# Exact key and query parts in the zeroed rows of the first attention's score products, doubled by transfers

## The reference, cut to what matters

```
def step(state, inp):
    qt, kt, vt, gt = inp
    gate = jnp.exp(gt)
    state = state * gate[..., None] + vt[..., None] * kt[..., None, :]
    out_t = jnp.einsum('bhvk,bhk->bhv', state, qt)
    return (state, out_t)
```

## Time and profile before

| | |
|---|---|
| median of 3 runs | 3458.81 us (3458.78 to 3458.85) |
| the profiled execution | 3460.7 us, span of its trace 3459.0 us |
| PE busy | 3342.5 us, 97% of the span |
| DVE busy | 2607.4 us, 75% |
| ACT busy | 1863.8 us, 54% |
| POOL busy | 1273.4 us, 37% |
| DMA engines | 11.3% on the main queue |

### The profile page before, as it was taken

The page is one execution under the profiler, slowest core; times in us unless marked ns, Lnnn a source line. Parts: engine busy times, 40 slices in busy tenths (PEclk is TensorE's granted clock), DMA queues, the critical chain, the costliest instruction groups (busy, mean ns, idle before and its releaser), DMA issues.

```text
span 3459.0 us, 88576 instructions
## 1 busy us (share of the span) xinstructions
PE 3342.5 (97%) x34556; PEld 2274.0 (66%) x34556; DVE 2607.4 (75%) x6329; ACT 1863.8 (54%) x4135; POOL 1273.4 (37%) x1393
## 2 busy tenths in 40 slices
PE   6999999999999999999999999999999999999998
PEld 3676666766666666666666666666676666766666
DVE  6777867778677777877778777786777867778777
ACT  3364654646546465463655636456364653646546
POOL 4424244242442524325233342423434244242442
PEclk8999999999999999999999999999999999999999
DMA  4001010010110101011010100101001010010110
GB/s 105 18 22 47 24 38 19 24 44 24 38 23 24 40 24 47 14 38 26 24 50 11 50 18 20 49 12 49 18 23 45 24 38 23 20 44 24 38 23 26
DMA packets 98479, 109.59 MB, mean 32 GB/s; under 512 B 21153, under 2 KB 75025, under 8 KB 98065
## 3 DMA queue, kind: packets, MB, share of 16 engines
q1 hardware_dynamic: 93200, 102.25, 11.3%
q10 hardware_dynamic: 4864, 1.69, 0.2%
HBM read 74.01 MB, written 17.30 MB: 26 GB/s over the span
## 4 chain that ended last, share of the span: by engine, by line
PE 75%; DVE 12%; ACT 5%; issue 5%; POOL 1%; DMA 0%; DVEq 0%; SPq 0%; ACTq 0%; POOLq 0%
PE bank L1549 6%; PE bank L1508 5%; PE bank L1879 5%; PE bank L1647 5%; PE bank L1529 5%; PE bank L1781 5%; PE bank L1897 4%; PE bank L1719 4%; PE bank L1664 3%; PE bank L1619 3%; PE bank L1816 3%; PE bank L1842 3%; PE bank L1604 3%; PE bank L1713 2%; DVE am L1245 2%
## 5 line engine op out<-in xcount | busy, mean ns | idle before, releaser
L867 POOL TENSOR_TENSOR qx<-qx 128x512 f32<-128x512 f32 x256 | 277.3, 1088 | 658.7 <-ACT qx L1113 657.8
L1470 DVE TENSOR_TENSOR sq_lo<-qx,sq_hi 128x512 fp32r<-128x512 f32 x256 | 224.1, 875 | 177.1 <-ACT sq_hi L1092 176.6
L1378 DVE TENSOR_REDUCE row_max<-bank 128x4 f32<-128x384 f32 x512 | 270.8, 550 | 95.4 <-PE bank L1781 95.0
L1245 DVE TENSOR_TENSOR am<-bank,causal 128x512 f32<-128x512 f32 x512 | 328.1, 683 | 11.3 <-PE bank L1619 11.3
L988 ACT ACTIVATE tanh_g<-bank 128x256 f32<-128x256 f32 x128 | 49.3, 385 | 394.9 <-PE bank L1508 394.9
L1508 PE MATMUL bank<-w_vg,xt 128*128 128x512 f32 x512 | 252.3, 615 | 0.0
L1549 PE MATMUL bank<-xt,w_down 128*128 128x512 f32 x512 | 237.2, 596 | 0.0
L1897 PE MATMUL bank<-sq_hi,pj_t 128*128 128x512 f32 x512 | 213.2, 416 | 14.8 <-DVE sq_lo L1470 10.3
L1387 DVE TENSOR_TENSOR am<-bank,row_max 128x384 f32<-128x384 f32 x384 | 212.8, 554 | 9.8
L1113 ACT ACTIVATE qx<-bank,scale_fc 128x512 f32<-128x512 f32 x256 | 177.9, 695 | 70.9 <-PE bank L1884 69.0
L1032 ACT ACTIVATE am<-am 128x384 f32<-128x384 f32 x384 | 202.9, 528 | 8.5 <-DVE am L1387 8.5
(11 more groups left out here) (264 smaller groups left out, 8671.4 us busy)
## 6 DMA issues: line engine op xcount, KB each, us to landing
g_wide<-gate_rows SPq DMA_DIRECT2D x64, 512.0 KB, 6.0
x<-in_L_attn_x SPq DMA_DIRECT2D x128, 128.0 KB, 2.3
qt<-in_L_attn_x SPq DMA_DIRECT2D x128, 128.0 KB, 2.6
out<-x SPq DMA_DIRECT2D x128, 128.0 KB, 1.7
k<-k SPq DMA_DIRECT2D x96, 128.0 KB, 2.4
qt<-in_L_attn_x ACTq DMA_DIRECT2D x8, 128.0 KB, 7.6
x<-in_L_ffn_w_fc SPq DMA_DIRECT2D x1, 1024.0 KB, 5.9
attn<-in_L_ffn_w_proj SPq DMA_DIRECT2D x1, 1024.0 KB, 8.7
```

The lines of the kernel that those rows point to most:

```text
L867: nc.gpsimd.tensor_tensor(sq[:, n % 3, :], relu[:, n % 3, :], relu[:, n % 3, :], ALU.mult)\
L1245: nc.vector.tensor_tensor(am_tiles[:, :, j], bank[3 + j][:].rearrange("p (f e t) -> p f e t", f=2, e=2), causal[:].unsqueeze(1).unsqueeze( ...
L1378: nc.vector.tensor_reduce(row_max[:, j, :], bank[1 + j][:, 0:4 * KW].rearrange("p (h k) -> p h k", k=KW), AX.X, ALU.max, negate=(j == 0)). ...
L1470: nc.vector.tensor_tensor(sq_lo[:, n % 3, :], sq[:, n % 3, :], sq_hi[:, n % 3, :].bitcast(F32), ALU.subtract)\
```

## The change

**Scores.** For chunks 1 to 7 the score product is no longer a float32 product with zeros. Keys and queries are split into a high part (rounded to float32r, which TensorE multiplies in one pass) and a low part (the rest, again rounded). Two tiles, `stacked` (the storage of `sq_hi` and `sq_lo`, free in this stage), hold for each chunk three 128x512 parts: `[0]` keys, `[1]` high queries, `[2]` low queries, each twice (`e`, once per head parity). In the copy for one parity, the 16 rows of the other head, which would hold zeros, are overwritten by transfers from the 16 rows next to them: the low keys (`k_low`) into part 0, the same queries into parts 1 and 2. One product over 32 rows then gives (high key + low key) . query part. There are 32 products of 128x128 in float32r for a chunk, instead of 8 of 128x256 in float32. Chunk 0 keeps the old way.

**Work for it.** ACT: `split_highs(c)`, two casts of 128x512. DVE: `split_queries(c)`, one subtraction of 128x512. POOL: `split_keys(c)`, one subtraction of 128x256; `parity_queries` remains for chunk 0 only. SP: `split_moves(c)`, 16 transfers of 16 rows each. PE waits for all 16 (`split_done`). Chunks 1 and 2 are split in chunk 0 (chunk 1's casts just before it), chunk c + 2 in chunk c.

**Seams.** ACT applies an exponential to one column (`warm`) before the last `experts_relu(3)`. DVE's `attention_bias(c-1)` moves for c = 1 and 2 ahead of the last `maxima` and `shifted`. POOL's `head_rstd` moves from after n = 4, 7 to after n = 5, 8, and DVE's normalising from n = 6, 7, 8, 9 to 6, 7, 9, 10.

```diff
-    qp = qx_flat[:, 0:8 * P].rearrange("p (b f e t) -> p b f e t", b=2, f=2, e=2)
+    qp = qx_flat[:, 0:4 * P].rearrange("p (f e t) -> p f e t", f=2, e=2)
+    k_low = qx_flat[:, 4 * P:8 * P].rearrange("p (b f t) -> p b f t", b=2, f=2)
+    stacked = tuple(tile[:].rearrange("p b t -> p (b t)").rearrange("p (i e f t) -> p i e f t", i=3, e=2, f=2)
+                    for tile in (sq_hi, sq_lo))
@@ SP
+                    def split_moves(c):
+                        sp.wait_ge(s["spq_ok"], at("spq_ok", c))
+                        sp.wait_ge(s["spk_ok"], at("spk_ok", c))
+                        tile = stacked[c % 2]
+                        for e in range(2):
+                            for j in range(4):
+                                here = slice(32 * j + DH * e, 32 * j + DH * e + DH)
+                                there = slice(32 * j + DH * (1 - e), 32 * j + DH * (1 - e) + DH)
+                                sp.dma_start(tile[there, 0, e].bitcast(F32), k_low[here, c % 2]).then_inc(split_done[c], 16)
+                                sp.dma_start(tile[there, 1:3, e].bitcast(F32), tile[here, 1:3, e].bitcast(F32)).then_inc(split_done[c], 16)
                     for g in range(NG):
+                        if g:
+                            for c in range(1, 4):
+                                split_moves(c)
...
+                    for c in range(4, NC):
+                        split_moves(c)
@@ POOL
+                    def split_keys(c):
+                        pool.wait_ge(s["sph_ok"], at("sph_ok", c))
+                        nc.gpsimd.tensor_tensor(k_low[:, c % 2].bitcast(F32R), kt[:, :, c * P:(c + 1) * P],
+                                                stacked[c % 2][:, 0, 0].bitcast(F32), ALU.subtract)\
+                          .then_inc(s["spk_ok"], 1)
-                            parity_queries(c + 1)
+                            if c == 0:
+                                split_keys(1)
                             hidden_gated(c + 1)
+                            if c + 2 < NC:
+                                split_keys(c + 2)
-                        if n in (4, 7):
-                            head_rstd(pool, n // 7)
+                        if n in (5, 8):
+                            head_rstd(pool, n // 8)
@@ ACT
                     experts_relu(2)
+                    nc.scalar.activation(warm[:], gdiff[:, 0:1], ACT.Exp)
                     experts_relu(3)
+                    def split_highs(c):
+                        if c >= 3:
+                            act.wait_ge(s["at_ok"], at("at_ok", 4 * c - 4))
+                        cols = slice(c * P, (c + 1) * P)
+                        nc.scalar.copy(stacked[c % 2][:, 1], qt[:, :, cols].unsqueeze(1).broadcast_to([P, 2, 2, P]))
+                        nc.scalar.copy(stacked[c % 2][:, 0], kt[:, :, cols].unsqueeze(1).broadcast_to([P, 2, 2, P]))\
+                          .then_inc(s["sph_ok"], 1)
+                    split_highs(1)
                     for c in range(NC):
+                        if c + 2 < NC:
+                            split_highs(c + 2)
@@ DVE
+                    def split_queries(c):
+                        dve.wait_ge(s["sph_ok"], at("sph_ok", c))
+                        nc.vector.tensor_tensor(stacked[c % 2][:, 2],
+                                                qt[:, :, c * P:(c + 1) * P].unsqueeze(1).broadcast_to([P, 2, 2, P]),
+                                                stacked[c % 2][:, 1].bitcast(F32), ALU.subtract).then_inc(s["spq_ok"], 1)
                         if c + 1 < NC:
                             experts_gate(c)
+                        if c == 0:
+                            split_queries(1)
+                        if c + 2 < NC:
+                            split_queries(c + 2)
...
+                        if 0 < c < 3:
+                            attention_bias(c - 1)
                         maxima(4 * c + 7)
                         shifted(4 * c + 7)
-                        if c:
+                        if c >= 3:
                             attention_bias(c - 1)
@@ PE, parity_scores(c)
-                        pe.wait_ge(s["qx_ok"], at("qx_ok", c + 1))
+                        if c == 0:
+                            pe.wait_ge(s["qx_ok"], at("qx_ok", 1))
+                        else:
+                            pe.wait_ge(split_done[c], at("split_done", 16 * 16))
...
+                        tile = stacked[c % 2]
                         for half in range(2):
-                            for j in range(4):
...
+                            for e in range(2):
+                                for part in range(2):
+                                    for j in range(4):
+                                        rows = slice(32 * j, 32 * j + 32)
+                                        mm = nc.tensor.matmul(bank[3 + j][:, (2 * half + e) * P:(2 * half + e + 1) * P],
+                                                              tile[rows, 0, e, half, :], tile[rows, 1 + part, e, half, :],
+                                                              start=(part == 0), stop=(part == 1), skip_group_check=True)
```

More of the change, by code:

```diff
@@ L113, in build_program @@
     gden = sb("gden", [P, NC])
+    warm = sb("warm", [P, 1])
     g_top = sb("g_top", [P, 2, NC])
@@ L303, in build_program @@
     low_banks = (2, 0)
+    split_done = [sem(f"split_done{c}") for c in range(NC)]
     x_in = [sem(f"x_in{c}") for c in range(NC)]
@@ L327, in build_program @@
             (128, "xc_ok"),
+            (256, "split_done"),
     ):
@@ L1481, in _ @@
                             head_moments(dve)
[L1482 to L1484 removed]
+                        if n in normalise_steps:
+                            p = normalise_steps.index(n)
+                            head_normalise(dve, 2 * p)
+                            head_normalise(dve, 2 * p + 1)
                         if n == NG * MT - 2:
```

45 lines of the change are left out of this document (22 added, 23 removed).

## The result

| | before | after |
|---|---|---|
| median of the runs (least to most), us | 3458.8 | 3724.7 (3721.2 to 3726.6) |
| ratio after/before, 95% interval | | 1.077 (1.075 to 1.079) |
| span of the profiled execution, us | 3459.0 | 3724.4 |
| mean granted clock | 1.00 | 0.96 |
| a sequence, first score product to first score product, us | 212.08 | 228.62 |

The change costs 266 us, 16.6 in each of 16 sequences. I had forecast slower, but 106 us: the direction was right, and the time lies above my range (3690). First the page of the kernel after. The second line is its chain of waits by engine.

What follows compares the result with a forecast made beforehand. PE's nearly gapless list was taken as the bound. Chunk 1 later by 5.0, clock 2.2 and seams -0.6 gave +6.6 us a sequence, +106 us over 16: 3565 us, 8 in 10 between 3495 and 3690.

Steps and rivals of the forecast that it cites:

- products, casts, subtractions: Score products and added work on ACT, DVE and POOL: no gain or loss, 0 us a sequence.
- chunk 0 to 1 longer: PE stands 5.8 us for SP's 16 transfers before chunk 1, which starts 5.0 us later than before.
- slow clock in chunk 1: The clock falls to 1.2 GHz after PE's gap before chunk 1, costing 2.2 us more a sequence.
- chunks 2 to 7: Later batches land before PE needs them, so these chunks lose nothing.
- seams: Waits of PE removed by `warm` (0.76 us) and by moving `attention_bias` and `head_rstd` (0.6 us) a sequence.
- No stall, 2.3 us spare: In steady state chunk 7's data are there 17.0 us after chunk 5 began; chunks 5 and 6 last 19.26.
- so the size does not matter: SP issues 16-row and 128-row transfers alike in 0.46 us, so the batch's last issue starts 6.9 us later.
- rival 1: SP also bounds later chunks at 0.65 us an issue: 13.7 us a sequence, 3678 us; chance 0.12.
- The mechanism at chunk 1: Batch released after `f_gates` and DVE's subtraction, issued by SP over 6.9 us, landing 2.1 us later; PE stands 5.8 us.
- The gain of 0.7 us a chunk: Score products at 56 ns each would gain about 0.7 us in each of 7 chunks; the forecast took 0.

Runs made afterwards that it cites:

- no transfers: The changed kernel without the 112 transfers a sequence that double the parts; casts, subtractions and short products stay: 3432.4 us, ratio 0.992.
- seams alone: The kernel before with only the edits to `warm`, `attention_bias`, `head_rstd` and `head_normalise`, score products as before: 3426.3 us, ratio 0.991.
- the kernels with small transfers: Two variants of the changed kernel, each batch's transfers replaced by small ones from DRAM and SBUF into an unread tile: 3666.5 and 3665.0 us, one run each.
- the kernel with chunk 1 as before and keys first: The changed kernel with chunk 1's scores made like chunk 0's and POOL's `split_keys(c + 2)` ahead of `hidden_gated(c + 1)`: 3546.7 us, ratio 1.025.
- eight transfers: The changed kernel with only the queries' parts transferred, 8 issues a batch instead of 16, two thirds of the bytes: 3517.8 us, ratio 1.017.
- 9 filling products: The changed kernel with 9 unused float32 products of 512 columns on PE before its wait for chunk 1's transfers: 3699.6 us, ratio 1.068.

## Why the prediction was wrong, step by step

All terms in us for a sequence; the measured ones are from the table of distances.

| step | predicted | measured |
|---|---|---|
| products, casts, subtractions | 0 | +0.4 (no transfers against seams alone: 6 us in 16; contained in the rows below) |
| chunk 0 to 1 longer | 5.75 (5.0 after the seam's 0.76) | 8.78 |
| slow clock in chunk 1 | 2.2 | 2.58 (2.45 come back when filled) |
| chunks 2 to 7 | 0 | 7.35 |
| seams | -1.36 (0.76 and 0.6) | -2.16 |
| sum | 6.6 | 16.55 |

**The step that failed most: "No stall, 2.3 us spare".** 7.35 of the missing 10 us are there. It had three faults. I released each batch by DVE's subtraction, and did not follow POOL's queue: the keys' subtraction for chunk 5 stands behind `hidden_gated(4)`, which in this order cannot start before ACT's rectifier at the end of chunk 3. That order was in the list of instructions, and the release at chunk 4's start + 1.2 us would have given a stall even at 0.46 an issue (1.2, 6.9 and 2.1 are 10.2, against the 9.3 of chunk 4: 0.9 us). Moved to the front, it gives back 2.3 us. SP's batch was 7.4 us in my sum and is 10.3 to 10.9, longer than a chunk of 9.6. And my sum had no term for the gate loads in SP's list, 3.1 us between the batches of chunks 3 and 4, which make PE wait for chunk 4 as soon as the first stall is gone. That a stall at chunk 5 also takes the clock with it (chunk 5 to 6, +1.73) follows from the same omission.

**The second: "so the size does not matter", 0.46 us an issue.** The rows and bytes didn't matter in the kernels with small transfers either, but I drew the value from DRAM transfers and set aside the only row with transfers inside SBUF, the key copies of 0.60, with an explanation (2 KB rows) that no row supported. 15 times 0.18 is 2.7 of the 3.0 us by which chunk 1 came later than I said; 0.2 is its release. My rival 1 had this price, 0.65, and its terms (7.9, 2.4, 4) come nearer than the forecast's; I gave it 0.12. It too lacks POOL's queue, and ends at 3678.

**What held.** The mechanism at chunk 1: released by DVE after chunk 0's `f_gates`, issued one by one by SP, landed 2 us later, PE standing. The clock: the 9 us gap does what the one of 4.5 did, 2.6 us are lost behind it. The Trainium skill's page "DMA: Bandwidth & Descriptors" ("Issuing engines are not separate DMA queues") calls the time to initiate a DMA usually small beside the transfer. For one of these transfers the issue is 0.6 of the 2.0 us until it has landed; for 16 behind one another the issues take 9.6 us and the last landing 2.1, so for the batch the measurement decides against it. The products: 32 of 128 columns run in 1.11 us where 16 records took 1.15, each row group's eight 0.12 apart from start to start, near the loads' 0.115. The gain of 0.7 us a chunk, an estimate from the 56 ns for a product by itself in the Trainium skill's page "TensorE: Matmul & The Clock Gate", section "Back-to-back issue gap", didn't come: between chunks 2 and 3, where nothing else interferes, the kernel without transfers gains 0.04 against the seams alone. The seams were undersized by 0.8 us; 0.25 of it is waits that I had counted only in part.

## What to carry to other kernels

Count the transfers, not their bytes, when one queue issues them, and take the price of an issue from a row with the same kind of source and destination: here 0.64 us (0.68 as a mean) within SBUF, so 16 of them outlast a chunk of 9.6 us. Count everything else in that queue too, here the gate loads. A stall that is taken away can uncover another behind it, as the one before chunk 4. A batch is released by the last of its producers, and each producer's own queue must be followed through whatever stands before it, here through POOL to ACT's last rectifier of the chunk. A stall of PE was paid twice here, by its length and by a slow clock behind it: 2.6 us behind the 8.8 before chunk 1, and still about 0.9 behind the 2.1 before chunk 4 in the kernel with chunk 1 as before and keys first. And work that is moved to another engine's queue can cost there what it saves: half of the issues on POOL gave back 69 us, where I had expected at least 160.

## What was not expected of the hardware

- An issue of a transfer from SBUF to SBUF took SP 0.59 to 0.60 us, from DRAM to SBUF 0.42 to 0.43, for 16 or 128 rows; the former was the same for rows of 32 bytes and of 2 KB. By turns they took 0.51 and 0.58. From SBUF to DRAM (`out`) it took 0.33.
- POOL issued the keys' transfers, from SBUF to SBUF, in 0.48 us each.
- Single issues on SP took up to 1.8 us in the kernel after, which lifts the mean step from 0.64 to 0.68. Why is open.
- PE's waits of 3.4 to 4.6 us before chunk 1 with eight transfers were each time followed by a slow chunk (12.4 to 14.1 us, against 11.1 at full clock). Of three waits of 1.4 to 1.6 us there with 9 filling products, two were (12.5) and one was not (10.8); those under 1.1 us were followed by 10.8 to 11.4.
